# Spreading a head's source-score row inside the preceding head's second step, in a graph attention kernel

## The reference

```
h = (x @ W).reshape(N, H, C)
al_s = einsum('nhc,hc->nh', h, a_src)        # source scores
al_d = einsum('nhc,hc->nh', h, a_dst)        # destination scores
e = leaky_relu(al_s[src] + al_d[dst], 0.2)
m = segment_max(e, dst);  ex = exp(e - m[dst])
alpha = ex / (segment_sum(ex, dst)[dst] + 1e-16)
out = segment_sum(h[src] * alpha, dst) + bias
```

## Time and profile before

| | us |
|---|---|
| median of 3 runs | 1061.52 |
| lowest and highest run | 1061.0, 1066.12 |
| the profiled execution's own time | 1066.05 |
| span in the profile | 1064.2 |
| TensorE busy in the span | 932.1 (88%) |
| VectorE busy | 645.0 (61%) |
| ScalarE busy | 395.0 (37%) |
| GpSimd busy | 224.2 (21%) |

### The profile page before, as it was taken

One profiled execution on the slowest core, in us unless ns is written; L12 is line 12 of the kernel. 1 busy time (PEld: TensorE's weight loads), 2 busy tenths in 40 slices (PEclk: granted clock), 3 DMA queues, 4 the chain that ended last, 5 costly groups with the idle time before them and its releaser, 6 DMA issues.

```text
span 1064.2 us, 14315 instructions
## 1 busy us (share of the span) xinstructions
PE 932.1 (88%) x4770; PEld 791.1 (74%) x4770; DVE 645.0 (61%) x1334; ACT 395.0 (37%) x553; POOL 224.2 (21%) x113
## 2 busy tenths in 40 slices
PE   0387678997999999999999999997999999379996
PEld 0155346666878788877888778877999999379996
DVE  8775656838998735775459645535222121897874
ACT  1643333125665146631665226634111111622220
POOL 6000200021452024410444003330000000243431
PEclk9998899999999999999999999999999999589998
DMA  3006991504001630036100540125111100101122
GB/s 119 32 1 128 152 208 60 172 7 126 30 29 44 223 131 29 29 116 241 41 29 30 164 147 30 50 100 220 68 52 64 41 36 1 44 15 58 58 61 70
DMA packets 38588, 86.62 MB, mean 81 GB/s; under 512 B 17131, under 2 KB 17291, under 8 KB 36912
## 3 DMA queue, kind: packets, MB, share of 16 engines
q1 hardware_dynamic: 38543, 86.03, 27.5%
HBM read 64.27 MB, written 21.76 MB: 81 GB/s over the span
## 4 chain that ended last, share of the span: by engine, by line
issue 38%; PE 30%; DVE 13%; POOL 7%; ACT 6%; DMA 4%; DVEq 1%; POOLq 0%; SPq 0%; ACTq 0%
PE ps L1218 7%; PE ps L1220 7%; PE ps L1219 7%; POOL prow L409 5%; PE ps L1250 4%; POOL W1lo L618 2%; DMA hidden_scratch<-ebuf 2%; DVE junk_w L1011 2%; DVE ring L1023 2%; DMA a2row<-in_L_gnn_att_dst 1%; DVE oh_lo L983 1%; DVE src_f L911 1%; PE ps L1326 1%; PE ps L1262 1%; ACT prow L404 1%
## 5 line engine op out<-in xcount | busy, mean ns | idle before, releaser
L409 POOL TENSOR_TENSOR prow<-prow,arow 125x1250 f32<-125x1250 f32 x50 | 139.3, 2788 | 648.1 <-ACT prow L404 648.1
L1218 PE MATMUL ps<-hhi,PThi 125*125 125x512 f32 x400 | 161.8, 404 | 1.0 <-DVE hlo L998 1.0
L1219 PE MATMUL ps<-hlo,PThi 125*125 125x512 f32 x400 | 158.1, 395 | 0.0
L1220 PE MATMUL ps<-hhi,PTlo 125*125 125x512 f32 x400 | 157.7, 394 | 0.0
L415 ACT ACTIVATE prow<-prow,expb 125x1250 f32<-125x1250 f32 x50 | 67.0, 1340 | 173.2 <-POOL prow L409 152.1
L1218 PE MATMUL ps<-W2p,hT 128*125 128x384 f32 x320 | 110.5, 345 | 7.5 <-DVE W2p L1104 5.6
L1220 PE MATMUL ps<-W2p,hT 128*125 128x384 f32 x320 | 108.5, 339 | 0.0
L1219 PE MATMUL ps<-W2p,hT 128*125 128x384 f32 x320 | 108.4, 339 | 0.0
L1063 DVE TENSOR_TENSOR hT<-ps,hT 128x500 fp32r<-128x500 f32 x40 | 25.3, 674 | 128.3 <-ACT hT L775 123.6
L1023 DVE TENSOR_SCALAR ring<-table,ekey 125x420 bf16<-125x420 uint16 (+1 forms) x240 | 69.4, 351 | 53.2 <-PE ps L1250 48.4
L466 PE MATMUL ps<-ident,prow 125*125 125x125 f32 x500 | 68.2, 287 | 28.1 <-DVE prow L446 11.8
(11 more groups left out here) (156 smaller groups left out, 1804.8 us busy)
## 6 DMA issues: line engine op xcount, KB each, us to landing
xr<-xT_scratch SPq DMA_DIRECT2D x30, 750.0 KB, 4.4
hidden_scratch<-ebuf SPq DMA_DIRECT2D x40, 250.0 KB
hblk<-hidden_scratch SPq DMA_DIRECT2D x10, 1000.0 KB
xT_scratch<-xa SPq DMA_DIRECT2D x20, 375.0 KB, 12.8
w1raw<-in_L_gnn_W SPq DMA_DIRECT2D x4, 1536.0 KB, 8.1
w1raw<-in_L_gnn_W SPq DMA_DIRECT2D x12, 512.0 KB, 3.5
w2late<-in_L_gnn_W SPq DMA_DIRECT2D x10, 384.0 KB, 8.0
xall<-in_x SPq DMA_DIRECT2D x5, 750.0 KB
```

The costliest lines, as they stand in the source:

```text
L409: pool.tensor_tensor(buf[:, s, :], buf[:, s, :], row, ALU.add).then_inc(e_done, 1)
L1218: pe.matmul(dst, ahi, bhi, start=start, stop=False)
L1219: pe.matmul(dst, ahi, blo, start=False, stop=False)
L1220: return pe.matmul(dst, alo, bhi, start=False, stop=stop)
```

## The change

The spreads of heads 1 to 3, and their copies, leave the place ahead of head 0. The row of head h + 1 is spread in step 1 of head h instead, for h = 0, 1, 2: on TensorE behind the transposes of row g + 1 and ahead of the matmuls of row g, on ScalarE at the end of the step. All three use set 1 of the PSUM banks. TensorE waits for the first copy, in place of the third, ahead of row 0's transposes. VectorE's wait for all copies ahead of head 0 is gone; a wait for the copy of the next head's row stands ahead of each `maxima` of the next head.

```diff
@@ ScalarE, ahead of head 0
             for j in range(HB, NB):
                 split_h(0, j, j % 2)
-            for h in range(1, H):
-                act.wait_ge(bc_ps, h + 1)
-                row_out(arow[:, H - 1 - h, :], h % 2).then_inc(bc_sb, 1)
             act_split(act, 0, 0, PThi)
@@ ScalarE, end of a step
                     if more(4) and not last:
                         act.wait_ge(t_done, g + 3)
                         scores(nxt(4)[0], nxt(4)[1], s)
+                    if h + 1 < H and isinstance(j, int) and j == 1:
+                        act.wait_ge(bc_ps, h + 2)
+                        row_out(arow[:, H - 2 - h, :], 1).then_inc(bc_sb, 1)
@@ VectorE
             dve_split(dve, 1, 1, PThi, PTlo)
-            dve.wait_ge(bc_sb, H)
             dve.wait_ge(ld_b1, 16)
...
                     if h + 1 < H and isinstance(j, int) and 6 <= j < 9:
+                        dve.wait_ge(bc_sb, h + 2)
                         maxima(h + 1, j - 6)
@@ TensorE, ahead of head 0
-            for h in range(1, H):
-                if h >= 2:
-                    pe.wait_ge(bc_sb, h - 1)
-                spread(lambda b: al[:, h, b:b + 1], h % 2).then_inc(bc_ps, 1)
-            pe.wait_ge(bc_sb, 3)
+            pe.wait_ge(bc_sb, 1)
             pe.wait_ge(pc_done, 1)
             pe_transpose(pe, 0, 0, prow)
@@ TensorE, a step
                         pe_transpose(pe, g + 1, 1 - s, prow)
+                        if h + 1 < H and isinstance(j, int) and j == 1:
+                            spread(lambda b: al[:, h + 1, b:b + 1], 1).then_inc(bc_ps, 1)
```

## The result

| | before | after |
|---|---|---|
| median, us | 1064.03 (5 runs, 1061.0 to 1066.12) | 1071.71 (5 runs, 1068.45 to 1072.31) |
| ratio, 95% interval | | 1.0070 (1.0043 to 1.0096) |
| span of the profiled execution | 1064.2 | 1068.2 |

What follows compares the result with a forecast made beforehand. VectorE's list sets the start of head 0, TensorE the pace in heads 1 and 2, both nearly level in head 0. 0 + 2.2 + 2.28 + 2.28 = 6.8 us, giving 1068.3 us, 0.64% slower; range 1064.5 to 1071.5.

Steps and rivals of the forecast that it cites:

- Gain ahead of head 0: 0: Ahead of head 0, removing spreads and copies gains 0, as VectorE's unchanged list reaches row 0's split at the same time.
- the cancellation named: At row 0's transposes, a start 1.2 us earlier is eaten by the low clock: 2.42 us, not 1.25.
- The cushion named: Ahead of head 0's step 1, TensorE's 1.27 us idle for VectorE covers 2.5 us more of matmuls at half speed.
- The low clock: At row 0's transposes, the granted clock is 0.50 after some 6.7 us of TensorE idle, so they take 2.42 us.
- Added in heads 1 and 2: 2.28 each: In step 1 of heads 1 and 2, no TensorE idle covers the spread, so each pays 2.28 us in full.
- Head 0: 2.2: In step 1 of head 0, VectorE starts about 2.2 us later and never catches up; head 0 pays 2.2.
- ScalarE's copy hidden: In step 1, the copy of some 1.2 us is hidden by the next `act_exp`'s 3.12 us wait for GpSimd's add.
- Rival 2: Head 0 takes its spread at 1.0 us, and row 1's transposes at full clock gain 1.2: +4.4 us, chance 0.15.
- Rival 3: Ahead of head 0, GpSimd's earlier add holds VectorE's one-column operations, some 2.5 us late: 9.3 us slower, chance 0.12.
- Rival 1: Ahead of head 0, ScalarE's chain through spreads and copies saves up to 4.9 us: +1.9 us, no measurable change, chance 0.10.

Runs made afterwards that it cites:

- e2_none: The kernel before without the three spreads and copies of heads 1 to 3, which read head 0's source scores instead; ratio 0.9989 to before.
- e4_double: The changed kernel with every spread in the steps made twice; one run, 443.14 us from head 0's step 1 to head 3's last transposes, against 436.87.
- e3_warm: The changed kernel with three spreads that nothing reads put back on TensorE ahead of row 0's transposes; ratio 1.0086 to before.
- e6: The kernel before with the third spread behind row 0's transposes, its copy behind row 2's scores, and VectorE's row 0 split ahead of row 2's maximum; ratio 1.0030.
- e7: The kernel before with only VectorE's split of row 0 moved ahead of the maximum of row 2; ratio 1.0024 to before.
- e0_after: The changed kernel once more, unaltered, as reference on the chip of the next three runs; 1072.82 us, ratio 1.0077 to before.
- e1_add: The kernel before with one more spread in step 1 of heads 0, 1 and 2, which nothing copies out or waits for; ratio 1.0070.
- e5_late: The kernel before with its third spread moved between the transposes of rows 0 and 1, its copy ahead of row 2's scores; ratio 0.9999.
- e9: The kernel before with two GpSimd waits, the third spread behind row 0's transposes and its copy ahead of row 2's scores; ratio 0.9983.
- e8: The kernel before with two GpSimd waits, holding the adds of rows 1 and 3 for VectorE's work on rows 0 and 2; ratio 0.9984.

## Why the prediction was right

The direction, the size and the places are as forecast. The ratio is 1.0070 against 1.0064. The median, 1071.71, stands 0.2 us above the upper end of the range, because it was put on a median of before of 1061.52 from three runs, which five runs give as 1064.03; the forecast difference of 6.8 us is 7.4 by the ratio and 6.7 in the traces.

- *Gain ahead of head 0: 0.* Right, and by the cancellation named: row 0's transposes start 1.60 us after VectorE's mark and not 2.74, and take 2.44 us and not 1.25. VectorE reaches row 0's split 5.99 us after the mark in both. e2_none shows it for the removal alone. The cushion named for a clock that comes back later (1.27 us ahead of step 1) was needed, and in e2_none and e4_double nearly used up; with a smaller one step 1 would have come later.
- *The low clock.* The granted clock was 0.50 at both sets of transposes, after 7.62 us without TensorE work and after 3.61. The rule of the Trainium skill ("TensorE: Matmul & The Clock Gate", sections "Part 1" and "Part 4"), by which activity lifts the throttle and transposes do not count as such, agrees: row 0's transposes alone did not bring the clock back. In e3_warm, with spreads put back, row 0's transposes took 1.32 us. But the spreads ahead of them are no guarantee: in e6 and e7 the clock was low there, and these transposes took 2.06 and 2.16 us.
- *Added in heads 1 and 2: 2.28 each.* Step 1 is 10.29 us long in each, over 8.08: 2.21. The spread's price was read 0.07 too high; its end overlaps with what stands behind it (in head 0 the spread runs from 261.15 to 263.50, and the first matmul behind it starts at 263.25). From the step 1 of one head to that of the next the change costs 2.55, 2.09 and 2.08 us, which makes the 6.72.
- *Head 0: 2.2.* Measured 2.24 at once (270.35 - 259.98 = 10.37, over 8.13), 2.36 by step 9 and 2.55 by step 1 of head 1. VectorE had no idle time ahead of line 1074 of step 1; it now idles 2.10 us there (line 1073 in the changed kernel) until TensorE's matmuls end, and stays late. TensorE's wait for `PTlo` in head 0, 1.3 us before, was 1.0 and in e0_after 1.5: it absorbed nothing that can be told.
- *ScalarE's copy hidden.* All but some 0.3 us: it stands ahead of an idle time of 2.23 us that was 3.12. But the `act_exp` behind that idle time now starts 0.42 us after GpSimd's add has ended, in all profiles with the copy in this place that were looked at (after, e0_after, e3_warm), and 0.14 us after it in before and in e1_add, which has no copy. That was put at nothing; it fits the 0.2 us by which e1_add is less late at step 9. Its cause is open.
- *Rival 2* had two halves. Head 0 did not absorb. Its other half, 1.2 us for a clock that is up at row 1's transposes, came to 0.6 in e5_late, with new collisions beside it.
- *Rival 3.* Its mechanism is real, and its price of 2.5 us measures 2.1 in e3_warm. It did not strike because the clock was down. The Trainium skill ("GPSIMD Engine Reference", section "Key points") names the sharing that the held lines show.
- *Rival 1* followed the chain of waits. The chain did pass through the spreads, but where two branches end close together it shows one of them. VectorE's list, without a gap from the `hhi` to row 0's split, was the other. It has a gap further on: in before VectorE idles 2.35 us ahead of line 446 of row 2 (258.04), for ScalarE's exponential, which stands in ScalarE's list behind `act_split` of row 1 and so behind row 1's transposes. That is how their clock reaches step 1.

What stays open: when the clock falls and comes back. With the gap ahead of row 1's transposes left empty it was low there in all nine profiles (2.33 to 2.44 us); with a spread in the gap it was up in e5 and e6 and low in e9. One profile of each kernel does not show how often. The +0.3 us in layer 2 are scatter: in e0_after the same distance is 0.1 us shorter than before.

## What to carry to other kernels

Work moved from a stretch where an engine waits anyway to one where it sets the pace costs its full duration, however late it is needed: look up the idle time of that engine at both places first. Compare traces by distances from a mark just ahead of the change, not by spans. Before moving a GpSimd or VectorE operation by a microsecond, look at what of the other engine it will then run beside.

## What was not expected of the hardware

- Operations of VectorE that overlap a GpSimd add of 2.4 to 3.1 us can be held until it ends, whatever their size: 2.25 us for 125 x 1 numbers (alone 0.16), 4.01 us for line 431 (alone 1.46), 3.02 us for line 446 (alone 1.45); the two long ones ended 1.3 us behind the add. Not all are held: in e8 line 456, which reads PSUM, ran in 1.18 us inside the add of row 3.
- It works the other way too: in e7 the add of row 3 began 0.07 us after VectorE's line 431 and took 4.12 us, where it takes 2.88 in before.
- An early start on a slow clock was worth nothing here: 1.14 us earlier and 1.19 us longer.
